# Channel-statistics sums moved ahead of the even first stage, statistics ten steps ahead, in a fused group-norm and displaced-convolution kernel on one core

## The reference, cut to what matters

```python
x: (32, 384, 64, 64) float32; offset: (48, 2)
def reference(x, offset):
    g = x.reshape(32, 32, 12, 64, 64)             # group norm: 32 groups of 12 channels
    v = (g - mean(g)) / sqrt(var(g) + 1e-5)       # mean and variance over (12, 64, 64)
    # 48 positions, 8 channels each: shift by round(offset), zeros from outside,
    # then a depthwise 5 x 5 filter exp(-2 |tap + (offset - round(offset))|^2), normalised
    return x + depthwise_conv(displace(v, round(offset)), kernel(offset))
```

## Time and profile before

| what | value |
|---|---|
| median of 3 runs | 1196.63 us (1196.0 to 1199.26) |
| the profiled execution: time | 1197.39 us |
| its span, first to last instruction | 1195.6 us |
| PE busy | 1174.4 us (98%) |
| DVE, ACT, POOL busy | 912.0, 793.6, 973.5 us |
| granted clock of PE, mean | 0.998 |
| moved by DMA | 402.94 MB, 337 GB/s |

### The profile page before, as it was taken

The page is one execution under the profiler, slowest core; times in us unless marked ns, Lnnn a source line. Parts: engine busy times, 40 slices in busy tenths (PEclk is TensorE's granted clock), DMA queues, the critical chain, the costliest instruction groups (busy, mean ns, idle before and its releaser), DMA issues.

```text
span 1195.6 us, 114437 instructions
## 1 busy us (share of the span) xinstructions
PE 1174.4 (98%) x50736; PEld 1144.7 (96%) x50736; DVE 912.0 (76%) x1327; ACT 793.6 (66%) x921; POOL 973.5 (81%) x1741
## 2 busy tenths in 40 slices
PE   9899999999999999999999999999999999999997
PEld 9899999999999999999999999999999999999997
DVE  6687787777778778787777877777777787877773
ACT  3567666666766776667676666676666766667754
POOL 5787888879788888978878887887888888888884
PEclk9999999999999999999999999999999999999999
DMA  8599999999999999999999999999999999999956
GB/s 266 173 383 383 368 358 345 351 352 348 354 341 349 348 341 351 344 352 348 346 347 350 350 349 346 346 346 355 345 349 345 347 347 354 341 354 344 354 199 211
DMA packets 409761, 402.94 MB, mean 337 GB/s; under 512 B 16528, under 2 KB 409744, under 8 KB 409744
## 3 DMA queue, kind: packets, MB, share of 16 engines
q1 hardware_dynamic: 204944, 201.41, 51.6%
q10 hardware_dynamic: 204800, 201.36, 49.1%
HBM read 201.38 MB, written 201.33 MB: 337 GB/s over the span
## 4 chain that ended last, share of the span: by engine, by line
PE 87%; POOL 3%; issue 3%; ACTq 3%; ACT 1%; POOLq 0%
PE ps L658 57%; PE ps L669 27%; ACTq L605 2%; PE ps L650 2%; POOL t_full L255 1%; ACT x L599 1%; ACT ay L559 1%; POOL norm L316 1%; POOL rstd L300 1%; POOL xin L307 0%; POOL summands L274 0%; POOL summands L276 0%; POOL spread L296 0%; POOL var L298 0%; POOL inner L293 0%
## 5 line engine op out<-in xcount | busy, mean ns | idle before, releaser
L658 PE MATMUL ps<-ay,norm 32*128 32x128 f32 x24608 | 755.8, 274 | 8.8 <-ACT x L599 7.9
L658 PEld LDWEIGHTS ps<-ay,norm 32*128 32x128 f32 x24608 | 716.2, 187 | 18.3 <-issue 10.5
L581 ACT ACTIVATE y<-ps 128x1536 f32<-128x1536 f32 (+1 forms) x256 | 330.2, 1290 | 251.3 <-PE ps L658 251.3
L453 DVE BATCH_NORM_STATS2 stats<-xin 128x6 f32<-128x512 f32 x768 | 487.6, 692 | 3.3 <-DMA xin<-in_x_dram 3.3
L669 PE MATMUL ps<-ax,y 64*64 64x64 f32 x24576 | 404.0, 220 | 2.0 <-issue 2.0
L669 PEld LDWEIGHTS ps<-ax,y 64*64 64x64 f32 x24576 | 384.9, 135 | 19.1 <-issue 2.3
L481 DVE TENSOR_TENSOR xin<-ps,xin 128x1024 f32<-128x1024 f32 x256 | 313.5, 1224 | 89.0 <-PE ps L669 88.6
L316 POOL TENSOR_SCALAR norm<-xin,rstd,bias 128x768 f32<-128x768 f32 x256 | 260.7, 1020 | 121.5 <-PE ps L658 103.3
L307 POOL TENSOR_TENSOR xin<-x,xin 128x512 f32<-128x512 f32 x256 | 320.1, 1272 | 7.4 <-ACT x L599 7.2
L570 ACT ACTIVATE norm<-xin,bias,rstd 128x768 f32<-128x768 f32 x256 | 261.7, 1022 | 35.2 <-issue 34.5
L599 ACT ACTIVATE x<-ps 128x512 f32<-128x512 f32 x256 | 151.2, 591 | 83.4 <-PE ps L669 83.3
(11 more groups left out here) (58 smaller groups left out, 282.7 us busy)
## 6 DMA issues: line engine op xcount, KB each, us to landing
xin<-in_x_dram SPq DMA_DIRECT2D x512, 384.0 KB, 7.3
out_dram<-xin ACTq DMA_DIRECT2D x512, 384.0 KB, 7.4
off<-in_L_conv_offset_dram SPq DMA_DIRECT2D x1, 48.0 KB, 3.2
```

What stands on the lines that cost most here:

```text
L453: nc.vector.bn_stats(stats[:, s // PAIR % RING, s % PAIR, n, :], xin[:, s].rearrange("p (g q) f -> p q f g", g=GROUPS)[:, n]).then_inc(bn_ ...
L581: nc.scalar.activation(y[:, v].rearrange("p k r a m -> p a (k r) m")[:, 0:lanes], ps[:, v, 0:lanes, 0:POS * P].rearrange("p a (n m) -> p a ...
L658: last = nc.tensor.matmul(ps[:, v, a, P * k:P * (k + 1)], norm[rows, v, r, P * k:P * (k + 1)], ay[rows, k, r, :], start=(r == 0), stop=(r ...
```

## The change

`sum_stats(0)` leaves the even first stage and stands in front of it: PE does it after the second stages and after the waits for `x2_ready` and `result1_ready`, right before `begin_even`, and for the pair three ahead of the one just finished. POOL's `make_summands` of that pair moves ahead of `coefficients`. `LEAD` goes from 2 to 3, so `AHEAD` from 8 to 10: DVE's statistics run ten steps ahead. `FIRST` goes from 10 to 12. Ahead of the loop, the summands of pair 2 come early on POOL, PE sums them in the spare bank before the idle products, and DVE reduces them there after two calls of step 6; DVE then takes the statistics of steps up to 9 before its first step, where before it stopped at 7.

```diff
-LEAD = 2
+LEAD = 3
 AHEAD = PAIR * (LEAD + 2)
-FIRST = 10
+FIRST = 12
...
             make_summands(1, 1, early=True)
+            make_summands(2, 2, early=True)
             coefficients(1, 1, early=True, used=False)
-            make_summands(2, 2)
...
-                        coefficients(p + LEAD, (s // PAIR + LEAD) % 2)
-                    if not (tail and s // PAIR + LEAD + 1 >= STEPS // PAIR):
-                        make_summands(p + LEAD + 1, (s // PAIR + LEAD + 1) % RING)
+                        make_summands(p + LEAD, (s // PAIR + LEAD) % RING)
                     else:
                         pool.engine_nop().then_inc(summands_ready, PAIR)
+                    if not (tail and s // PAIR + LEAD - 1 >= STEPS // PAIR):
+                        coefficients(p + LEAD - 1, (s // PAIR + LEAD - 1) % 2)
...
-            sums(1, 1, early=True)
+            sums(1, 1, early=True, bank=1)
+            statistics(0, 6, 0)
+            statistics(0, 6, 1)
+            sums(2, 0, read=True, bank=1)
             nc.vector.engine_nop().then_inc(result1_ready, SPARE)
-            pair_statistics(0, 6, None, lambda: sums(LEAD, LEAD % 2, read=True, evicted=1))
+            statistics(0, 6, 2)
+            all_statistics(7)
+            pair_statistics(0, 8, RING, None)
...
-                            sums(p + LEAD + 1, (s // PAIR + LEAD + 1) % 2, read=True, evicted=t + PAIR)
+                            sums(p + LEAD, (s // PAIR + LEAD) % 2, read=True, evicted=t + PAIR)
...
                 y_product(1, 0)
-                pe.wait_ge(summands_ready, one)
-                sum_stats(0)
                 pe.wait_ge(mats_ready[2], one)
...
                 pe.wait_ge(result1_ready, two)
+                pe.wait_ge(summands_ready, two)
+                sum_stats(0)
                 begin_even(three)
...
             pe.wait_ge(first_summands, 2)
             sum_stats(1)
+            pe.wait_ge(first_sums, 2)
+            pe.wait_ge(first_summands, 3)
+            sum_stats(1)
             idle_products(2, 0)
```

More of the change, by code:

```diff
@@ L454, in statistics, with sums @@
                                    xin[:, s].rearrange("p (g q) f -> p q f g", g=GROUPS)[:, n]).then_inc(bn_done, 1)
-            def sums(pair, v, early=False, read=False, evicted=None):
+            def sums(pair, v, early=False, read=False, evicted=None, bank=0):
                 if read:
@@ L464, in sums @@
                     both[:, v].rearrange("p (t g) f -> p t (g f)", t=PAIR),
-                    ps[:, pair if early else 0, :, SUMS].rearrange("p a (t n e) -> p t e a n", t=PAIR, n=CHUNKS),
+                    ps[:, bank, :, SUMS].rearrange("p a (t n e) -> p t e a n", t=PAIR, n=CHUNKS),
                     AX.XY, ALU.add)
@@ L518, in step @@
                     reduced = None
-                    if not (tail and s // PAIR + LEAD + 1 >= STEPS // PAIR):
+                    if not (tail and s // PAIR + LEAD >= STEPS // PAIR):
                         def reduced():
-                            sums(p + LEAD + 1, (s // PAIR + LEAD + 1) % 2, read=True, evicted=t + PAIR)
+                            sums(p + LEAD, (s // PAIR + LEAD) % 2, read=True, evicted=t + PAIR)
                     else:
```

## The result

The changed kernel takes 1190.72 us (median of 8 runs, 1187.84 to 1193.62) against 1197.57 us of the kernel before in the same series (8 runs, 1196.00 to 1200.99): a ratio of 0.9943, with a 95% interval from 0.9926 to 0.9959. It is faster by 0.57%. The forecast of 1196.0 was wrong in its main step, and the first rival (1189.1 us) was right about that step; the time lies inside the range. Both were counted from a median of 1196.63; counted from this series' 1197.57 they would be 1196.9 and 1190.0.

A forecast was written before the change was run, and what follows sets the result against it. PE's own list was taken as the bound. The span of 1195.6 us, less 0.4 at the start, 0.2 at the end and 0 in the middle, gave 1195.0, or 1196.0 us against the median; range 1189.0 to 1200.5 us.

The forecast's parts named there:

- the first rival: Nothing holds PE to a rate, so all of (a) is gained: 1189.1 us; chance 0.25 for a gain over 3.6 us.
- (c): Second stages longer than in the last pairs, no releaser named: some 16 us, taken to fill up what (a) leaves.
- (a): PE's sums begin late because POOL makes the summands after the coefficients: 30 places, 6.9 us in all.
- (b): Superblock borders, where PE waits for ACT's copy of the last third: 7.6 us in 15 places.
- The place in front: Sums ahead of the even first stage instead of inside it: cost taken as 0, bounds 0.05 us a pair either way.
- the rival of a dearer place: Sums in front cost more than inside: at 0.3 us a pair 7 us more, 1203 us; chance 0.04.
- POOL's order: Summands ahead of coefficients: (a) goes, 0.3 us of slack in the worst pair; 0 of the 6.9 us taken for the time.
- Loads and stores: DVE's order: 24 us from a store's issue to the slot's next statistics, two medians 14.6 us; cost 0 in the middle.
- The rival of late loads: Loads come late up to about pair 15: 1 to 20 us, the middle giving 1206 us; chance 0.09.
- The start: Before the loop PE's wait of 1.87 us at 32.36 goes: second block 0.4 us earlier, loop begins at 31.3 us.
- The end: The last turn's sums move behind the last second stage, where ACT, DVE and stores end later anyway: 0.2 us less.
- The code: Four packets, 0.07 MB, on PE's instruction queue in the whole run: loop code brought once, not per pair.

The follow-up runs named there:

- POOL's order alone: The kernel before with one edit: POOL makes the summands of pair p + 3 ahead of the coefficients of pair p + 2; 1192.26 us, ratio 0.9949.
- the run with ten steps: The changed kernel with FIRST back from 12 to 10, so ten steps loaded at once; 1201.36 us, ratio 1.002.

## Why the prediction was wrong, point by point

- **The step that failed: that (c) fills up what (a) leaves.** I took PE to be held to some 9.04 us a pair, because superblocks with and without late sums had the same length: 24.95 us of second stages beside one with late sums, 25.69 beside one without, and equal averages over thirteen. That is a likeness of totals, and superblocks of one kernel scatter by more than the lateness in one (71.8 to 72.9 us before, 71.2 to 72.5 after, for 0.5 us of lateness). In that trace the six superblocks with more lateness do have 0.42 us less in their second stages than the seven others; but with no late sums at all (POOL's order alone) the stage grew by 0.014 us a pair only, 0.1 a superblock. What the runs show in its place: a late start of the sums costs its own length. The pair fell from 9.041 to 8.964 us, POOL's order alone gave 6.1 us by its ratio, and the doubled sums cost 0.20 us a pair for 0.22 of work. That a part of it comes back is not excluded (the interval of POOL's order alone is 4.4 to 7.9 us, the lateness 6.9). The prediction's own signs agree: superblocks of 71.7 us and second stages of 25.1 were to make the first rival right, and fourteen superblocks average 71.74 with 25.1. I had myself named the lack of a mechanism, and gave the rival 0.25. That the time still lies in the stated range is because the range took in the rival's case whole. The rule from "Trainium Architecture — The Big Picture" of the Trainium skill (it stands in the section "What this means for kernel authors": DMA and engines cannot contend for SBUF), by which the gain would stay, came to the right result here. What (c) is, this rule doesn't say: it goes with the issue of stores beside the loads' issue, and why is not shown.
- **(a), the size.** 6.9 us by 30 places; 0.057 us a pair, 6.7 us. Right.
- **(b), the borders.** I left them at 7.6 us. ACT's waits there fell to 4.4, the borders as a whole by 2.0 us. Their second stages are 0.22 us shorter each, their first stages 0.08 longer. That ACT's list sets the border, one run shows (the later store moved the wait). Why the halved stores took 2.4 of its 7.0 us, and what in the change shortened it, was not tested.
- **The place in front.** Taken as 0, with 0.05 us a pair either way: 8.762 us a free pair in both traces. Right, and the rival of a dearer place is out.
- **POOL's order.** The timeline of the pair of the earlier trace rows, after:

```profile
285.12 0.21 POOL L276 TENSOR_TENSOR summands<-stats 128x12 f32<-128x12 f32 x1 [0.15 <-POOL summands L274]
...
286.34 0.43 PE L654 MATMUL ps<-summands,ones 32*128 32x36 f32 x8
```

  The summands end at 285.33, 1.0 us before the sums, where I had counted 0.3 us of slack. The wait of up to 0.3 us in 15 places did not come.
- **Loads and stores.** 24 us for a store and a load were enough. DVE waits 2.43 us in the second pair and PE 0.72, where 2.72 and 0.80 stood, as forecast; there is no other wait for a load. The rival of late loads is out, though the run with ten steps shows how near it lay.
- **The start.** Forecast 0.4 us earlier, measured 2.4 later: a term left out of the sum. The wait was forecast (sums at 29.2; they stand at 29.47), but the loop begins at 33.38 and not at 31.3. What I left out is that it moved in front of the idle products, whose work is to keep PE busy: PE stood still for 1.65 us, its clock stayed at the lower level until 34.96, and the idle products took 1.7 us longer than ahead of the wait. With the order put right the first second stage begins at 34.75, 1.6 us earlier than before.
- **The end.** 0.2 us less forecast, nothing measured (19.35 us in both).
- **The code.** The four packets on PE's queue agree with a loop whose code is brought once, as I read. What I did not see is that PE waits for it in the first turn, for 1.25 us up to 40.17 in the kernel before.
- **The sum.** By measured terms: +2.4 at the start, -6.7 for (a), -2.0 for the borders, the rest -0.3: -6.6. That the time came close to the first rival's has a part of luck in it, as the start's loss took what the borders gave; neither term was in the forecast.

## What to carry to other kernels

Count a wait of the bound engine at its length until an experiment shows a hold: equal totals of neighbouring stretches are no evidence for one, when they scatter by more than the effect. When work is moved in a warm-up list, look at what each filler stands in front of and behind, since here 1.65 us without work was paid a second time by slower products behind it. Try the smallest part of a change alone: the swap of two calls on POOL gave what the whole change gave. And where a saving is real, look which engine's list is late next: 6 us were taken from inside the second stages, and 3.6 came back at their middle, most of it in one pair of eight, where ACT was late. The lowest time here has the change, the idle products first and the odd stores behind the copy: 1183.7 us, 1.2% under the kernel before, which can't be told from the idle products first alone (1.1%).

## What the runs showed of the hardware that I had not expected

- Products of the second stage, which wait for nothing in their records, start late when ACT issues two stores (1.4 us) from 0.3 us into the stage while SP issues loads: 11.9 us over the run in the kernel before, 0.125 us a stage where the two queues issue together for over 0.5 us and 0.01 where they don't. It is 2.4 us over the run with these stores issued 1.9 us into the stage, and 2.5 with half of their bytes, where SP's issues have left the stage too. Why the one hinders the other, no run shows.
- After 1.65 to 2.5 us without work at the start, PE's products took 1.4 to 1.9 times as long for several microseconds (3.75 against 2.03 us for 64, 5.46 against 3.83 for 128), at a granted clock between 0.50 and 0.72 where the trace has records of it. Yet in the kernel before, 1.87 us without work had no slow products behind it, while 1.88 us in the run with POOL's old order had them. The first 320 products of every trace run at the lower level too (18.8 a microsecond; 36 at the full clock).
- In the first turn of its loop PE stops, and goes on 1.2 to 1.6 us after the end of a 16 KB packet on its instruction queue, in all traces in which it stops there: 1.25 us in the kernel before, 2.52 and 0.99 with sixteen loads at once.
